# A two-layer AdaLN and FFN kernel: perceptron, attention and aggregated kernels computed beside the last unit, residual rows added by later transfers, the opening in a new order

## The chip, the core and the metric

The kernel is one launch on one core of a Trainium2 chip. The engines run side by side from their own instruction streams: TensorE (PE, with its weight loads shown as PEld), VectorE (DVE), ScalarE (ACT), GpSimd (POOL) and SyncE (SP). SP, ACT and POOL also issue DMA transfers; in the rows their queues are SPq, ACTq and POOLq. Each stream is executed in its own order, and streams wait for each other through semaphores. The metric is the device time of the launch in microseconds (us).

## What is computed

Only what matters here, from the reference; `x` is (32, 64, 1024), 32 batch entries of 64 channels of 1024 values.

```python
# layer 0, condition: grouped 1-d convolution, 9 taps, 4 groups, plus a term per batch entry and channel
out = conv(x, weight, groups=4) + (c @ c_weight.T)[:, :, None] + bias[None, :, None]
# layer 0, FFN on the 2048 rows of 1024: weights are 4-bit codes, looked up and scaled, plus a low-rank part
y1 = x1 @ w_up + b_up + x1 @ w_up_lora_a @ w_up_lora_b
y2 = relu(y1) @ w_down + b_down + relu(y1) @ w_down_lora_a @ w_down_lora_b
# layer 1, condition: a perceptron on the condition gives 8 attention weights per batch entry
h = gelu(embedding @ W0 + b0); h = gelu(h @ W1 + b1); att = softmax(h @ W2 + b2)
agg_w = einsum('bk,koi->boi', att, weight);  agg_b = att @ bias_k
out = einsum('boi,bih->boh', agg_w, x) + agg_b[:, :, None]
# layer 1, FFN: each row goes to the expert (of 8) with the highest gate
yj = xf @ expert_w[j].T + expert_b[j]
```

Layers also add their input (the residual); the kernel holds that sum in `acc`. The perceptron, its attention and the aggregated kernels `agg_w` depend on the condition alone, not on `x`. Their first use is layer 1's mixing of the channels, after the whole FFN of layer 0.

## The kernel before

**Opening.** PE computes the 32 convolutions (one per batch entry, `conv`), each into one of four banks; ACT writes the high part of the result (`conv_high`) and DVE the low part (`conv_low`). Convolution k may start when the low part of k-4 is done. Eight convolutions make one chunk of 512 rows: `stages[0]` to `stages[3]`, the last being the buffer `ring`. POOL stores each finished chunk to DRAM (`store_x1`: 8 transfers of 512 KB, 4 MB in all), since later units read it again. SP loads the inputs of the convolutions in pairs (`load_pair`, 516 KB, into four buffers).

**Weights.** In the same stretch the first weight tiles are decoded. Tile n is a `head` and seven `ramps` on ACT, seven additions on DVE (`add_ramps`), a multiplication by the scales `am` (`scale`), an addition of the low-rank product that PE makes (`lora_product`, `add_lora`), a rounding on ACT (`high`) and a subtraction on DVE (`low`). SP loads codes, scales and low-rank rows (`load_codes`, `load_scales`, `load_lora`); each buffer is loaded again once its last use is past, and SP waits for that in its own order. Tiles 0 and 1 are the "up" tiles of unit 0, tiles 2 and 3 its "down" tiles.

**Main part.** There are 11 units; the 2048 rows are 4 chunks. `up(q)` is 48 products of 128x512 for one chunk, `relu` and `hidden_low` turn its result into hidden values, `down(q)` is another 48 products in four parts j = 0 to 3. DVE adds each part to `acc` (`add_down`), and part j may start when the sum of part j-2 is made (semaphore `acc_added`). PE's order is up(q+1), down(q), up(q+2), and so on. `acc` lies on the memory of `stages[1]` and `stages[2]`. In the kernel before, POOL loads the residual rows `x_nat` into `acc` first (`load_rows`, 16 transfers of 512 KB), once the stage beneath has been used and stored, and `add_down` of unit 0 waits for them (`acc_in`).

**Condition of layer 1.** The ten constants are loaded by ACT's queue at the start. `perceptron(0)` to `perceptron(4)` and eight products `aggregate(j)` stand between convolutions 3 to 15, `aggregated(j)` on ACT copies each result out, and POOL stores the kernels (`batch_kernels<-aggs`, 512 KB). `aggs` and `kerns` lie on `stages[2]`: hence ACT waits for `aggs_stored` before it writes convolution 16.

**After the units** come the mixing of 16 row tiles (`z_product`, with blocks `bdg` loaded from the stored kernels), the gates, the routing and the experts.

The order of all of it is written out by hand, engine by engine, with one loop (`rounds`) for the repeating units. Before the change PE's order in the opening is convolutions 0 to 15, up(0), 16 to 23, up(1), 24 to 31, down(0).

## Time and profile before

| what | value |
|---|---|
| median of 3 runs | 1533.24 us (1530.97 to 1535.55) |
| the profiled execution's own time | 1532.94 us |
| its span in the trace | 1531.5 us |
| PE busy | 1431.8 us, 93% |
| DVE busy | 1125.8 us, 74% |
| ACT busy | 762.1 us, 50% |
| mean granted TensorE clock | 0.974 |
| bytes moved | 331.29 MB, mean 216 GB/s |

Of the 1532.94 us, 1.4 us lie around the span. A busy share is an average over stages; the stages differ, so the profile is read stage by stage. "Idle before" in a row is how long the engine stood still before the instruction, and the name behind the arrow is what ended that wait. A granted clock of 1.00 is 2.4 GHz, of 0.50 it is 1.2 GHz; a value between is a mean over a stretch.

### The profile page before, as it was taken

The page shows a single profiled execution, that of the slowest core. Times are in us where ns is not written, and L with a number is a line of the kernel's source. Part 1 is how long each engine was busy: PE and PEld are TensorE (multiplying, and loading weights), DVE is VectorE, ACT ScalarE, POOL GpSimd, SP SyncE. Part 2 cuts the span into 40 slices and gives each one's busy share as a digit, 9 for nine tenths or more (in the row PEclk, how much of TensorE's full clock was granted, in tenths as well). Part 3 has the DMA queues.
Part 4 walks back from the last instruction along what each step waited for, and adds up shares of the span by engine and source line. Part 5 has one row for each costly group of instructions (what it writes and reads, how often), then busy time and mean ns, then how long its engine had stood idle before and what let it go on. Part 6 is the DMA issues. An engine that isn't in the chain of part 4 may idle for free.

```text
span 1531.5 us, 20837 instructions
## 1 busy us (share of the span) xinstructions
PE 1431.8 (93%) x6815; PEld 1163.4 (76%) x6815; DVE 1125.8 (74%) x1075; ACT 762.1 (50%) x845; POOL 155.1 (10%) x215
## 2 busy tenths in 40 slices
PE   6886899999999999999999999999999499999896
PEld 5576788888888888888888888888865377777674
DVE  3672787877888788787887878875244588888885
ACT  3561554464455455445445445542112266776663
POOL 0112200000000000000000000000011233343440
PEclk8898999999999999999999999999999599999998
DMA  5567565755665665575565566466555845968860
GB/s 163 201 203 277 220 219 219 264 216 194 261 232 193 233 248 199 217 270 189 215 255 223 204 235 254 186 232 212 225 197 211 272 132 138 338 167 248 307 183 2
DMA packets 104365, 331.29 MB, mean 216 GB/s; under 512 B 17361, under 2 KB 24921, under 8 KB 104249
## 3 DMA queue, kind: packets, MB, share of 16 engines
q1 hardware_dynamic: 80478, 258.22, 45.2%
q0 software_dynamic: 22512, 71.32, 15.3%
q8 instruction: 54, 0.88, 0.2%
q10 hardware_dynamic: 1298, 0.68, 0.2%
q14 instruction: 23, 0.18, 0.0%
HBM read 295.04 MB, written 46.14 MB: 223 GB/s over the span
## 4 chain that ended last, share of the span: by engine, by line
PE 82%; DVE 5%; DMA 4%; ACT 3%; issue 3%; ACTq 1%; POOL 1%; DVEq 0%; SPq 0%; POOLq 0%
PE pair L1072 24%; PE pair L1074 23%; PE pair L1073 23%; PE pair L1121 3%; DVE wlr L1046 2%; PE pair L1216 2%; DMA am<-am_dn 1%; PE pair L1281 1%; DMA batch_kernels<-aggs 1%; PE pair L1131 1%; DVE wf L775 1%; ACT whr L707 1%; PE pair L1223 1%; DMA zg<-z_rows,zidx 1%; PE pair L1134 1%
## 5 line engine op out<-in xcount | busy, mean ns | idle before, releaser
L775 DVE TENSOR_TENSOR wf<-wf,term 128x1024 f32<-128x1024 f32 x308 | 377.2, 1225 | 93.4 <-ACT term L568 74.5
L568 ACT ACTIVATE term<-codes 128x1024 f32<-128x1024 int32 x308 | 321.0, 1055 | 107.0 <-DVE wf L775 107.0
L1072 PE MATMUL pair<-wh,hh 128*128 128x512 f32 x704 | 275.2, 391 | 4.0 <-DVE acc L814 2.6
L1074 PE MATMUL pair<-wh,hl 128*128 128x512 f32 x704 | 274.7, 390 | 0.0
L1073 PE MATMUL pair<-wl,hh 128*128 128x512 f32 x704 | 274.6, 390 | 0.0
L1072 PE MATMUL pair<-ring,wh 128*128 128x512 f32 x656 | 255.5, 390 | 1.5 <-issue 1.5
L814 DVE TENSOR_TENSOR acc<-acc,pair 128x1024 f32<-128x1024 f32 x176 | 214.2, 1217 | 57.9 <-PE pair L1074 57.7
L1074 PE MATMUL pair<-ring,wl 128*128 128x512 f32 x656 | 255.2, 389 | 0.0
L1073 PE MATMUL pair<-ring,wh 128*128 128x512 f32 x656 | 255.2, 389 | 0.0
L596 ACT ACTIVATE wh<-wf 128x1024 fp32r<-128x1024 f32 x44 | 46.7, 1060 | 338.7 <-DVE wf L790 338.7
L1046 DVE TENSOR_TENSOR wlr<-wraw,whr 128x1024 fp32r<-128x1024 f32 x184 | 213.1, 1219 | 2.8 <-ACT whr L707 2.8
L707 ACT ACTIVATE whr<-wraw 128x1024 fp32r x184 | 187.9, 1056 | 33.9 <-PE pair L1074 30.7
L1072 PE MATMUL pair<-whr,zth 128*128 128x512 f32 x368 | 151.4, 412 | 21.7 <-DVE wlr L1046 21.7
L1072 PEld LDWEIGHTS pair<-wh,hh 128*128 128x128 f32 x704 | 132.3, 188 | 31.6 <-DVE acc L814 2.7
L1073 PEld LDWEIGHTS pair<-wl,hh 128*128 128x128 f32 x704 | 132.2, 188 | 27.8
L1074 PEld LDWEIGHTS pair<-wh,hl 128*128 128x128 f32 x704 | 132.1, 188 | 27.6
L1073 PE MATMUL pair<-wlr,zth 128*128 128x512 f32 x368 | 144.6, 393 | 0.0
L1072 PEld LDWEIGHTS pair<-ring,wh 128*128 128x128 f32 x656 | 123.1, 188 | 28.1 <-issue 2.7
L1074 PE MATMUL pair<-whr,ztl 128*128 128x512 f32 x368 | 144.4, 392 | 0.0
L1073 PEld LDWEIGHTS pair<-ring,wh 128*128 128x128 f32 x656 | 123.1, 188 | 25.6
L1074 PEld LDWEIGHTS pair<-ring,wl 128*128 128x128 f32 x656 | 123.1, 188 | 25.5
L804 DVE TENSOR_TENSOR hl<-pair,hh 128x1024 fp32r<-128x1024 f32 x44 | 53.9, 1225 | 82.4 <-ACT hh L607 82.4
(165 smaller groups left out, 1386.8 us busy)
## 6 DMA issues: line engine op xcount, KB each, us to landing
ring<-x_parts SPq DMA_DIRECT2D x320, 512.0 KB, 7.7
wraw<-exp_w SPq DMA_DIRECT2D x64, 512.0 KB, 13.1
x_parts<-stage POOLq DMA_DIRECT2D x24, 512.0 KB, 8.5
xg<-exp_b POOLq DMA_DIRECT2D x23, 512.0 KB, 6.9
codes<-codes_up SPq DMA_DIRECT2D x22, 512.0 KB, 7.6
codes<-codes_dn SPq DMA_DIRECT2D x22, 512.0 KB, 6.2
am<-am_dn SPq DMA_DIRECT2D x22, 512.0 KB
acc<-x_nat POOLq DMA_DIRECT2D x16, 512.0 KB, 10.7
```

The lines of the kernel that those rows point to most:

```text
L568: return nc.scalar.activation(out, codes[:, n % 2], ACT.Relu, scale=scale, bias=-scale * bend)
L596: nc.scalar.activation(high_part(n), whole(n), ACT.Copy).then_inc(wh_ready, 1)
L707: nc.scalar.activation(whr[:, kt % 4], wraw[:, bass.ds(buf, 1), kt].rearrange("p a n -> p (a n)"), ACT.Copy).then_inc(whr_ready, 1)
L775: nc.vector.tensor_tensor(whole(n), whole(n), term[:, e % 2], op).then_inc(term_added, 1)
L804: nc.vector.tensor_tensor(hl[:, h:h + 2], pair[0][:].rearrange("p (s t) -> p s t", s=2), hh[:, h:h + 2], ALU.subtract).then_inc(hl_ready, 1)
L814: nc.vector.tensor_tensor(a, a, pair[2 + j % 2][:], ALU.add).then_inc(acc_added, 1)
L1046: nc.vector.tensor_tensor(wlr[:, kt % 4], wraw[:, bass.ds(buf, 1), kt].rearrange("p a n -> p (a n)"), whr[:, kt % 4], ALU.subtract).then_i ...
L1072: mm(ps, ah, bh, start=first, stop=False)
L1073: mm(ps, ah, bl, start=False, stop=False)
L1074: return mm(ps, al, bh, start=False, stop=last)
L1121: ins = mm(whole_bank[:, :, g * GC:(g + 1) * GC], xcv[h][p % 4][:, k % 2, g, d:d + P], tz[h][:, d, g], start=False, stop=g == GROUPS - 1 a ...
L1216: ins = mm(bank[4 * (p % 2) + h], bdg[:, p % 2], rows, start=True, stop=True)
```

## The change

It has four parts.

1. The perceptron, the attention and the aggregated kernels leave the opening. Their constants are loaded by SP near the end of the last decoded tile, the steps stand between the ups and downs of the last unit, the eight products stand two by two behind the four parts of the last unit's down(2), and POOL stores the kernels while down(3) runs. SP loads the first `bdg` blocks only after that store, between the rows 0 to 7 and 8 to 15 of the stores of `acc`.
2. `acc` is no longer loaded with `x_nat` ahead. In unit 0 DVE copies the first four downs into `acc`, and POOL then adds each row tile with an accumulating transfer (`accum_op=ALU.add`), one per finished copy; `add_down` of q = 4 waits for it.
3. The opening's order: convolutions 0 to 20, up(0), convolutions 21 to 23, up(1) with the low-rank product of tile 3 inside, 24 to 31, down(0). The decoding of tiles 0 to 3 is spread over it accordingly.
4. SP's loads in the opening follow that order; the low-rank rows and the scales of tile 3 now stand ahead of the loads of the last four pairs instead of behind.

```diff
-            load_rows(0) ... load_rows(3)      # acc[:, t] <- x_nat, after up_mm and x1_stored
+            for c in range(NC):
+                store_x1(c)
+            for t in range(TILES):
+                pool.wait_ge(acc_added, t + 1)
+                pool.dma_start(acc[:, t], x_nat[t * P:(t + 1) * P], accum_op=ALU.add).then_inc(acc_in[t // CT], 16)
...
-            act.wait_ge(aggs_stored, 16)
-            for k in range(HB, HB + CB):
+            for k in range(FIRST, LATE):
                 conv_high(k)
...
+            sp.wait_ge(term_ready, NCH * WT)
+            for dst, src in ((cta[:], cond_t), (w0s[:], w0), (b0s[:], b0), (w1s[:], w1), (b1s[:], b1), (w2s[:], w2),
+                             (b2s[:], b2), (kernb[:], kern_b), (gbs[:], gate_b)):
+                sp.dma_start(dst, src).then_inc(mlp_const, 16)
+            sp.wait_ge(dn_mm, TILES * (UNITS - 1))
+            sp.dma_start(kerns[:], kern).then_inc(kerns_in, 16)
...
+            store_rows(0)
+            store_rows(1)
+            sp.wait_ge(aggs_stored, 16)
             load_mixing(0, 0)
             load_mixing(0, 1)
+            store_rows(2)
+            store_rows(3)
...
             def add_down(i, q, j):
                 dve.wait_ge(dn_mm, i * 32 + 4 * q + j + 1)
+                a = acc[:, CT * (q % NC) + j]
                 if isinstance(i, int) and i == 0 and q < NC:
+                    dve.wait_ge(up_mm, 2 + q // 2)
+                    dve.wait_ge(x1_stored[1 + q // 2], 16 * KT)
+                    nc.vector.tensor_copy(a, pair[2 + j % 2][:]).then_inc(acc_added, 1)
+                    return
...
             for k in range(NC):
                 if k < NC - 1:
                     up(UNITS // 2, k + 1).then_inc(up_mm, 1)
-                down(UNITS // 2, k)
+                    perceptron(2 * k)
+                down(UNITS // 2, k, aggregates=k == 2)
+                if k < 2:
+                    perceptron(2 * k + 1)
```

How the orders differ at the places that matter. A name such as `early_xcv` is the input of a convolution, `x8` a repeated row. First PE in the opening, convolutions 8 and 9 of the kernel before with what stands around them:

```order
L1096 MATMUL pair<-ident,satt 8x32 [waits mlp_dve]
L1117 MATMUL pair<-ctxd,ones 128x512 [waits x1l_ready,ctxd_ready,xcv_in0]
L1121 MATMUL pair<-tz,xcv 128x8x16 x8
L1099 MATMUL pair<-att_t,kernb 128x32 [waits att_ready]
L1117 MATMUL pair<-ctxd,ones 128x512 [waits x1l_ready]
L1121 MATMUL pair<-tz,xcv 128x8x16 x8
L1105 MATMUL pair<-kerns,att_t 32x512 [waits aggb_ready]
```

and the same convolutions in the changed kernel:

```order
L1129 MATMUL pair<-tz,early_xcv 128x8x16 x8
L1125 MATMUL pair<-ctxd,ones 128x512 [waits x1l_ready,ctxd_ready,xcv_in0]
L1129 MATMUL pair<-tz,xcv 128x8x16 x8
L1125 MATMUL pair<-ctxd,ones 128x512 [waits x1l_ready]
L1129 MATMUL pair<-tz,xcv 128x8x16 x8
L1125 MATMUL pair<-ctxd,ones 128x512 [waits x1l_ready,xcv_in1]
```

Between convolutions PE no longer waits for attention (`satt`, `att_t`, `aggb`). Second, SP's queue before, from the last load of the first 12 pairs to the loads for tile 4:

```order
L304 DMA early_xcv<-x_conv 128x1032 [waits conv_mm]
L366 DMA tz<-toep 128x1024 [waits x1_stored0,up_mm]
L317 DMA lora_raw<-lora_dn_at 96x128 [waits lora_ready]
L304 DMA xcv<-x_conv 128x1032 [waits conv_mm]
L304 DMA late_xcv<-x_conv 128x1032 [waits conv_mm] x3
L310 DMA codes<-codes_up 128x1024 [waits term_ready]
L327 DMA am<-am_dn 128x1x1024 [waits scaled]
L317 DMA lora_raw<-lora_up_b 96x128 [waits lora_ready]
```

and in the changed kernel:

```order
L310 DMA early_xcv<-x_conv 128x1032 [waits conv_mm]
L333 DMA am<-am_dn 128x1x1024 [waits scaled]
L323 DMA lora_raw<-lora_dn_at 96x128 [waits lora_ready]
L333 DMA am<-am_dn 128x1x1024 [waits scaled]
L376 DMA tz<-toep 128x1024 [waits x1_stored0,up_mm]
L310 DMA xcv<-x_conv 128x1032 [waits conv_mm]
L310 DMA late_xcv<-x_conv 128x1032 [waits conv_mm] x3
L316 DMA codes<-codes_up 128x1024 [waits term_ready]
```

The scales of tile 3 (the second `am_dn`) moved from behind the pairs of the last chunk to ahead of them. Third, ACT beside the last unit in the changed kernel, from `relu(1)` to the first of the mixing; before, the same stretch holds the `relu` groups alone:

```order
L612 ACTIVATE pair<-pair,bup 128x512
L617 ACTIVATE hh<-pair 128x1024 [waits relu_done,dn_mm]
L563 ACT_TABLE_LOAD
L563 ACTIVATE hid<-pair,b0s 128x32 [waits mlp_mm]
L566 ACTIVATE hid<-pair,b1s 128x32 [waits mlp_mm]
L612 ACTIVATE pair<-pair,bup 128x512 [waits up_mm]
L612 ACTIVATE pair<-pair,bup 128x512
L617 ACTIVATE hh<-pair 128x1024 [waits relu_done,dn_mm]
L569 ACT_TABLE_LOAD
L569 ACTIVATE satt<-pair,satt 32x8 [waits mlp_dve]
```

The perceptron's steps now stand behind `relu`, and the table load for each stands ahead of the instruction that waits. On PE, the step that needs the attention, between up(3) and down(2) of the last unit:

```order
L1079 MATMUL pair<-ring,wl 128x512
L1106 MATMUL pair<-att_t,kernb 128x32 [waits att_ready]
L1077 MATMUL pair<-wh,hh 128x512 [waits acc_added,hl_ready,wl_ready]
```

Before, the products of down(2) follow those of up(3) with nothing between.

## Rows read from the trace of the kernel before

**Rows 1.** Busy time by stage: us, busy us of each engine, clock, DMA share, GB/s.
```profile
0.00:78.85 78.85, 56.24 (x320) 45.36 (x320) 39.13 (x51) 36.50 (x55) 7.43 (x21) 0.87 0.57 186
78.85:157.28 78.43, 61.72 (x373) 55.63 (x373) 37.61 (x41) 32.02 (x44) 11.00 (x21) 0.87 0.64 225
201.00:1052.00 851.00, 849.54 (x3810) 703.79 (x3809) 684.39 (x605) 435.56 (x489) 0.31 (x1) 1.00 0.60 226
```

**Rows 2.** The chain of work that ended last, in the opening: start, us, what.
```profile
71.85 0.97 PE pair L1105 x2
...
80.86 18.78 DMA batch_kernels<-aggs
...
114.97 22.23 DMA am<-am_dn
```

**Rows 3.** PE in order of time: start, duration, line, operation, idle before.
```profile
10.61 0.77 PE L1117 MATMUL pair<-ctxd,ones 128*128 128x512 f32 x1 [4.00 <-DVE ctxd L759]
...
14.13 0.48 PE L1117 MATMUL pair<-ctxd,ones 128*128 128x512 f32 x1
...
16.15 0.47 PE L1117 MATMUL pair<-ctxd,ones 128*128 128x512 f32 x1
```

**Rows 4.** PE, the same view: a wait for the perceptron, a low-rank product.
```profile
26.23 0.41 PE L1089 MATMUL pair<-hid,w1s 128*128 128x32 f32 x2 [3.55 <-ACT hid L553]
...
65.50 1.11 PE L1131 MATMUL pair<-lora_t,lora 96*128 96x128 f32 x8
```

**Rows 5.** PE, the same view: up(0), up(1), convolution 28, down(0).
```profile
78.85 0.79 PE L1072 MATMUL pair<-stage,wh 128*128 128x512 f32 x1 [0.68 <-ACT aggs L564]
...
91.89 0.39 PE L1117 MATMUL pair<-ctxd,ones 128*128 128x512 f32 x1
...
113.85 0.48 PE L1072 MATMUL pair<-stage,wh 128*128 128x512 f32 x1
...
124.87 0.39 PE L1117 MATMUL pair<-ctxd,ones 128*128 128x512 f32 x1
...
145.05 0.76 PE L1117 MATMUL pair<-ctxd,ones 128*128 128x512 f32 x1 [11.95 <-DVE ring L819]
...
157.28 0.50 PE L1072 MATMUL pair<-wh,hh 128*128 128x512 f32 x1 [1.41 <-DVE ring L819]
```

**Rows 6.** DVE in order of time, in the opening, columns as for PE.
```profile
80.92 1.23 DVE L775 TENSOR_TENSOR wf<-wf,term 128x1024 f32<-128x1024 f32 x1 [3.05 <-ACT term L568]
...
91.80 1.22 DVE L790 TENSOR_TENSOR wf<-wf,pair 128x1024 f32<-128x1024 f32 x1
...
138.55 1.22 DVE L790 TENSOR_TENSOR wf<-wf,pair 128x1024 f32<-128x1024 f32 x1
...
144.22 2.47 DVE L819 TENSOR_TENSOR ring<-pair,ring 128x512 fp32r<-128x512 f32 x4
```

**Rows 7.** Transfers by issue, 43 to 44 and 74 to 77 us: KB each, us to landing.
```profile
early_xcv<-x_conv SPq DMA_DIRECT2D x1, 516.0 KB, 7.8
...
early_xcv<-x_conv SPq DMA_DIRECT2D x1, 516.0 KB, 17.2
```

**Rows 8.** ACT and DVE in order of time, at `relu(2)` of the last unit.
```profile
1084.00 1.24 ACT L602 ACTIVATE pair<-pair,bup 128x512 f32<-128x512 f32 x2 [19.41 <-PE pair L1074]
1085.33 1.03 ACT L607 ACTIVATE hh<-pair 128x1024 fp32r<-128x1024 f32 x1
...
1087.53 1.21 DVE L814 TENSOR_TENSOR acc<-acc,pair 128x1024 f32<-128x1024 f32 x1
1089.34 1.22 DVE L814 TENSOR_TENSOR acc<-acc,pair 128x1024 f32<-128x1024 f32 x1 [0.60 <-PE pair L1074]
```

**Rows 9.** ACT in order of time: table load, first perceptron step.
```profile
24.59 1.28 ACT L553 ACT_TABLE_LOAD   x1
25.89 0.29 ACT L553 ACTIVATE hid<-pair,b0s 128x32 f32<-128x32 f32 x1
```

**Rows 10.** The page's transfers by issue: an accumulating one, KB each, median us to landing.
```profile
xg<-exp_b POOLq DMA_DIRECT2D x23, 512.0 KB, 6.9
```

More of the change, by code:

```diff
@@ L171, in program @@
         term = sb(late, "term", [P, 2, L])
+        cta = sb(tail, "cta", [P, P])
+        w0s = sb(tail, "w0s", [P, P])
+        w1s = sb(tail, "w1s", [P, P])
+        w2s = sb(tail, "w2s", [P, E])
+        b0s = sb(tail, "b0s", [P, 1])
+        b1s = sb(tail, "b1s", [P, 1])
+        b2s = sb(tail, "b2s", [1, E])
+        kernb = sb(tail, "kernb", [E, P])
+        hid1 = sb(tail, "hid1", [P, B])
+        hid2 = sb(tail, "hid2", [P, B])
+        satt = sb(tail, "satt", [B, 3 * E])
+        tail.close()
         codes = sb(late, "codes", [P, 2, L], I32)
@@ L345, in _ @@
             load_pair(1)
+            load_pair(2)
             load_lora(0, 0)
+            load_scales(0, 0)
+            load_pair(3)
             load_codes(0, 1)
-            load_scales(0, 0)
-            for p in range(2, 6):
-                load_pair(p)
+            load_pair(4)
             load_lora(0, 1)
+            load_pair(5)
             load_pair(6)
-            load_codes(0, 2)
             load_scales(0, 1)
             load_pair(7)
+            load_codes(0, 2)
+            load_pair(8)
             load_lora(0, 2)
-            load_pair(8)
             load_pair(9)
+            load_pair(10)
             load_codes(0, 3)
-            load_pair(10)
+            load_pair(11)
             load_scales(0, 2)
-            load_pair(11)
+            load_lora(0, 3)
+            load_scales(0, 3)
             sp.wait_ge(up_mm, 1)
@@ L613, in conv_high @@
                                      ACT.Copy).then_inc(x1h_ready, 1)
-            act.wait_ge(ffn_const, 32)
-            for k in range(HB):
+            for k in range(FIRST):
                 conv_high(k)
@@ L675, in _ @@
             high(UNITS // 2, 3)
-            for k in range(3):
-                relu(UNITS // 2, k + 1)
+            relu(UNITS // 2, 1)
+            perceptron(0)
+            perceptron(1)
+            relu(UNITS // 2, 2)
+            perceptron(2)
+            relu(UNITS // 2, 3)
+            for j in range(8):
+                aggregated(j)
             act.wait_ge(aggb_ready, 2)
@@ L808, in add_down @@
                 dve.wait_ge(dn_mm, i * 32 + 4 * q + j + 1)
+                a = acc[:, CT * (q % NC) + j]
                 if isinstance(i, int) and i == 0 and q < NC:
-                    dve.wait_ge(acc_in[q], 16 * CT)
-                else:
-                    dve.wait_ge(acc_added, i * 32 + 4 * (q - NC) + j + 1)
-                a = acc[:, CT * (q % NC) + j]
+                    dve.wait_ge(up_mm, 2 + q // 2)
+                    dve.wait_ge(x1_stored[1 + q // 2], 16 * KT)
+                    nc.vector.tensor_copy(a, pair[2 + j % 2][:]).then_inc(acc_added, 1)
+                    return
+                if isinstance(i, int) and i == 0:
+                    dve.wait_ge(acc_in[q - NC], 16 * CT)
+                dve.wait_ge(acc_added, i * 32 + 4 * (q - NC) + j + 1)
                 nc.vector.tensor_tensor(a, a, pair[2 + j % 2][:], ALU.add).then_inc(acc_added, 1)
@@ L820, in conv_low @@
                                         stages[c][:, :, 0, col:col + CH], ALU.subtract).then_inc(x1l_ready, 1)
-            for k in range(HB):
+            for k in range(FIRST):
                 conv_low(k)
@@ L866, in _ @@
             add_lora(0, 2)
+            low(0, 2)
             dve.wait_ge(up_mm, 1)
@@ L870, in _ @@
             hidden_low(0, 0)
-            for k in range(HB, HB + CB):
+            for k in range(FIRST, LATE):
                 conv_low(k)
-                if k < HB + 7:
-                    add_ramps(0, 3, (k - HB + 1,))
-                if k == HB + 1:
-                    lora_low(0, 3)
-                    low(0, 2)
+            add_ramps(0, 3, (1,))
+            lora_low(0, 3)
+            add_ramps(0, 3, range(2, 8))
             scale(0, 3)
@@ L881, in _ @@
             hidden_low(0, 1)
-            for k in range(HB + CB, B):
+            for k in range(LATE, B):
                 conv_low(k)
@@ L910, in _ @@
                     hidden_low(UNITS // 2, k + 1)
+                if k == 1:
+                    perceptron(0)
+                    perceptron(1)
+                elif k == 2:
+                    perceptron(2)
+                    perceptron(3)
                 for j in range(CT):
@@ L1157, in up, with down @@
                 return ins
-            def down(i, q, between=None):
+            def down(i, q, between=None, aggregates=False):
                 pe.wait_ge(wl_ready, i * 8 + 4 * (q // 4) + 4)
```

200 lines of the change are left out of this document (77 added, 123 removed).

## The prediction, made before the changed kernel had run

> **What bounds the kernel now.** I read the busy time by stage first. From 201 us on PE is busy without a gap and at full clock, for 850 us of a main part that the change leaves alone, and the same holds up to 1127 us [rows 1]. The opening is different: in its two halves PE is busy for 56.2 of 78.9 and 61.7 of 78.4 us, at a granted clock of 0.87, and DVE and ACT are below half [rows 1]. No engine bounds the opening; waits do. So I read the chain of waits there. Two single transfers hold 41.0 us of it: the store of the aggregated kernels (18.8 us), for which ACT waits before convolution 16, and the scales of tile 3 (22.2 us) [rows 2]. The second ends in PE standing still for 11.95 us before convolution 28 [rows 5]. Before those two, PE waits for the perceptron between convolutions, as the 3.55 us at 26.2 us [rows 4]. The goal of the reading is one time: down(0) of unit 0 starts at 157.28 us [rows 5]. From there both kernels have the same order of work on PE, DVE and ACT, until the last unit.
>
> **The opening, step by step.** The costs: the first convolution takes 14.13 - 10.61 = 3.5 us, a later one 16.15 - 14.13 = 2.02 us [rows 3]; a low-rank product of the up kind 1.1 us [rows 4]. DVE needs 0.62 us for a low part (2.47 for four) and 1.22 us for one operation on a weight tile [rows 6], 1.84 us together, and the new order gives it one such operation per convolution: PE's 2.02 us is the longer. The start hardly moves: ACT issues ten transfers less, but the convolution also needs its input, and I take 10.5 us instead of 10.61.
> Convolutions 0 to 20 then end at 10.5 + 3.5 + 20 x 2.02 + 2 x 1.1 = 56.6 us. I add 1.5 us for a late input (below): 58.1.
> up(0) needs the low part of tile 1, which now comes last: after convolution 20 one ACT copy and three DVE operations (0.6 + 0.6 + 2 x 1.2 with the hand-overs), 3.8 us. PE stands still for that, so up(0) starts slowly, as it did before: 91.89 - 78.85 = 13.0 us with its slow start and one low-rank product [rows 5]. It ends at 74.9.
> Convolutions 21 to 23: 6.1, to 81.0. `relu(0)` and its low part are done by then (74.9 + 3.6, the time from `relu` to the first addition in [rows 8]), so up(1) runs at once: 124.87 - 113.85 = 11.0, plus 0.5 for the product inside, to 92.5 [rows 5]. Convolutions 24 to 27 need nothing more: to 100.6.
> Convolution 28 needs the low part of 24, and DVE is the later one there. Tile 3: ACT writes convolution 23 and the head and first ramp of tile 3 by 83.7; from the first addition to the end of `add_lora` it took 93.0 - 80.9 = 12.1 us for tile 2 with nothing between [rows 6], so 95.9; from there to the end of `hidden_low` 144.2 - 139.8 = 4.4, so 100.3, and 0.7 for the low part: 101.0. Convolutions 28 to 31 end at 109.1, and the last low part brings down(0) to 110.8 (before: 1.7 us behind the last convolution).
> **Term of the opening: 157.3 - 110.8 = 46.5 us less.** The 22 us wait for scales goes because SP now issues that load right behind `scale` of tile 2 (about 72 us), 22 us before it is needed and before the store of the next chunk; what is late next is DVE's tile 3, as computed.
>
> **The residual rows.** 16 plain loads leave (two groups of eight, one of them beside the late scales), and 16 accumulating ones come, one per copied tile, some 5.5 us apart. DVE's copy in place of the sum reads the same 1024 values; I cost it at nothing. The trace has one accumulating transfer of the same size, 6.9 us to landing [rows 10]. The last of a group is issued as its down ends; it is needed when the same rows come again four steps later, 3 x 22 us at least. So it is hidden by the main part; if it were not, `add_down(4)` would stall. POOL has nothing else queued there. Bounds: 0 to 3 us, for loads of the ring that it delays; I take 0.
>
> **The last unit.** Here PE has no gap, so what is put on it costs in full. Eight aggregated products at 0.97 us [rows 2]: 7.8. The perceptron's six small ones, from 0.1 to 0.4 us each: 1.2. Then waits. perceptron(0) and (1) find their inputs ready: ACT works them off beside a down or an up of 11 us, and the nine constants were issued a down and an up before. perceptron(4) stands between up(3) and down(2) and needs the attention that DVE copies after `hidden_low(3)`: `relu` to the first addition is 1087.5 - 1084.0 = 3.5 us [rows 8], plus the copy and the step: 3.9 us in which PE stands still, and then a slow start, priced by the two ups: 13.0 - 11.0 - 0.5 = 1.5 us [rows 5]. Behind it down(2), the `relu` after it and everything later wait. In down(1) DVE does the softmax between `hidden_low` and its first sum. Part 2 of down waits for that sum; it is ready at 1088.7 and wanted at 1089.3 [rows 8]. The softmax puts about 1.5 us in (two small operations, the exponential, two more), less 0.4 us by which PE is later itself: 0.5 us. The table load for the exponential (1.28 us [rows 9]) stands ahead of the waiting instruction, from 1086.3 on, beside `hidden_low`.
> In [rows 9] the instruction behind a table load starts 0.02 us after it. The Trainium skill (ScalarE: Activation LUTs, What ACT_TABLE_LOAD costs) counts a drain of 1.38 us on top, 2.66 us per switch. The row speaks against this; by the page the sum would be about 1.4 us higher.
> The kernels' store is issued behind the last aggregated product, while down(3) runs for 11 us. The 18.8 us that it took before had 4 MB of other stores ahead on the same queue; now nothing is ahead. With some 4 us, and 4 us for the blocks, it is hidden; bounds 0 to 8 us, I take 0.
> **Term of the last unit: 7.8 + 1.2 + 3.9 + 1.5 + 0.5 = 14.9 us more.**
>
> **Sum.** 1532.94 - 46.5 + 14.9 = 1501.3 us. The median of the runs, 1533.24, is 0.3 us above the profiled execution: 1501.5.
>
> **The rivals.**
> *The opening becomes short of transfers.* The first store of 4 MB now starts at about 30 us, and the pairs for convolutions 14 and 16 are issued at 34 to 35 us beside it. The pair for 14 is wanted at 41.3. Such a pair took 7.8 us beside the first store before and 17.2 beside the second [rows 7]: ready at 42 or at 51. I took 1.5 us, near the first row, since that one also was issued just behind a store's start. With the second PE would lose 10 us and 1.5 for the slow start: 1511.
> The Trainium skill (DMA: Bandwidth & Descriptors, Queues, rings and completion order) says that each DMA engine goes round-robin between queues, by packets. By that rule a pair would never wait for the whole store, and the 1.5 us would fall away; the 17.2 us row speaks against it.
> *The clock does not recover.* If convolutions with short waits keep PE at the mean 0.87 of now, 2.02 us becomes 2.3: 32 convolutions and two ups cost 12 us more, 1513. For it: waits of 1 to 2 us are followed by slow stretches now. Against it: from 14.13 us on, without waits, the pace is 2.02.
> *The accumulating transfers hold the main part up (slower than before).* Their place is the wait of `add_down(4)` to `(7)` in unit 0. Group 0 is wanted 3 x 22 = 66 us after its last issue, group 3 seven steps, 154 us, after down(0). If the sixteen went one behind another they would be late at all from 154 / 16 = 9.6 us each, and would eat the 31.6 us won from 11.6 us each; at 12.5 us each, 200 - 154 = 46 us late, 1547. For it: nothing in the trace shows sixteen of them in a row. Against it: one lands 6.9 us after its issue, beside other transfers, and transfers overlap.
> *The condition's work is not in the way before.* If DVE and ACT set the opening and not its waits, the gain is one of the two transfers only, some 22 us, with 15 given back: 1526. Rows 1 speak against it, both are half idle.
>
> **How the numbers follow.** Forecast (1494 to 1508) 0.68; short of transfers 0.12; clock 0.10; gain of one transfer only 0.04; accumulating transfers 0.04; nothing moves 0.02. The lower end is the forecast with no late input, a hidden softmax and no slow start, and a start 3 us earlier, and DVE 2 us quicker over tile 3: 1493. The upper end takes in the first two rivals and the 8 us of the store's bound in part: 1515. A measurement of this kernel tells 0.3% (4.6 us) from no change. Faster by more than that: all but the last two cases, 0.94; within: 0.02; slower: 0.04.
>
> **What would show it.** Down(0) starts near 111 us, at a clock above 0.95 in the first 58 us; no wait of DVE for `am`; no wait of ACT for `batch_kernels`; a gap of 3 to 4 us on PE ahead of perceptron(4) and a last unit longer by 15 us; DVE never waits for `acc`'s accumulating transfers. Wrong are I if PE waits for a pair of inputs at convolutions 14 to 20, if DVE is late at convolution 28 by more than a microsecond, or if the first `bdg` block comes after down(3).

## The result, and the profile after

| | median | runs |
|---|---|---|
| before | 1533.97 us | 4 (1530.97 to 1535.55) |
| changed | 1548.21 us | 4 (1546.64 to 1552.64) |

The ratio is 1.0100, with a 95% interval of 1.0074 to 1.0126: the changed kernel is 14 us slower. Forecast was 1501.5, with a range that ended at 1515. The profiled execution of the changed kernel took 1546.64 us, its span is 1545.2. All comparisons of places below are made in the spans, 1545.2 against 1531.5: 13.7 us. One of the four executions of the kernel before with the scales on 16 engines, an experiment below, took 2918.49 us and is left out of that kernel's median, 1510.03 us; two expectations still count it and write 1511.2.

The stages first (us; busy us of each engine, clock, DMA share, GB/s), beside [rows 1]:

```profile
0.00:66.44 66.44, 50.26 (x377) 48.56 (x377) 42.09 (x51) 36.38 (x50) 9.45 (x24) 0.95 0.72 260
66.44:124.23 57.79, 49.42 (x287) 43.63 (x287) 34.19 (x35) 26.01 (x34) 4.19 (x8) 0.91 0.49 174
125.00:250.00 125.00, 105.65 (x452) 84.80 (x451) 85.29 (x76) 52.93 (x59) 17.54 (x24) 0.96 0.85 235
250.00:1052.00 802.00, 799.98 (x3588) 663.22 (x3587) 637.19 (x564) 405.96 (x456) 0.31 (x1) 1.00 0.60 224
```

The opening is shorter and denser, and from 250 us on the main part runs without a gap as before. The third row is new: 19 us of PE are missing in the first 125 us of the main part, at a DMA share of 0.85 and yet only 235 GB/s. What PE waited for in the whole kernel (us in all, times, longest), the rows that concern the change. L1077 holds products of an up or a down, L1125 opens a convolution, L1222 is the mixing, L1106 the step that needs the attention:

```profile
PE pair L1077 <- DMA ring<-x_parts: 16.8, 7, 7.7
PE pair L1125 <- DMA xcv<-x_conv: 9.6, 2, 6.4
PE pair L1222 <- DMA bdg<-batch_kernels: 7.8, 1, 7.8
...
PE pair L1125 <- DMA early_xcv<-x_conv: 4.0, 1, 4.0
PE pair L1106 <- DVE att_t L746: 3.9, 1, 3.9
PE pair L1077 <- DVE wl L806: 3.7, 1, 3.7
```

Four of the six are transfers (3.2 of the 9.6 us are the first convolution's, at the start). In order of time on PE: convolution 14, up(0), up(1), convolution 24, down(0), beside [rows 5]:

```profile
44.73 0.80 PE L1125 MATMUL pair<-ctxd,ones 128*128 128x512 f32 x1 [4.01 <-DMA early_xcv<-x_conv]
...
66.44 0.51 PE L1077 MATMUL pair<-stage,wh 128*128 128x512 f32 x1 [3.68 <-DVE wl L806]
...
86.40 0.47 PE L1077 MATMUL pair<-stage,wh 128*128 128x512 f32 x1 [0.55 <-issue]
...
104.48 0.80 PE L1125 MATMUL pair<-ctxd,ones 128*128 128x512 f32 x1 [6.41 <-DMA xcv<-x_conv]
...
124.23 0.50 PE L1077 MATMUL pair<-wh,hh 128*128 128x512 f32 x1 [1.41 <-DVE ring L831]
```

The chain of work that ended last, its four longest transfers up to 260 us (start, us, what), beside [rows 2]:

```profile
33.80 10.88 DMA early_xcv<-x_conv
...
81.55 22.90 DMA xcv<-x_conv
...
173.45 27.18 DMA ring<-x_parts
...
207.84 27.54 DMA ring<-x_parts
```

Three transfers of half a megabyte took 23 to 28 us each, and they set the end. The difference of the two spans, by stage:

| stretch | before | changed | difference |
|---|---|---|---|
| start to down(0) of unit 0 | 157.28 | 124.23 | -33.0 |
| down(0) to `relu(1)` of the last unit (its `hh` copy at 1063.56 and 1053.65) | 906.28 | 929.42 | +23.1 |
| from there to the last sum into `acc` (1127.42 and 1133.59) | 63.86 | 79.94 | +16.1 |
| last sum to the end | 404.1 | 411.6 | +7.5 |
| sum | | | +13.7 |

In the last stretch the third `z` tile comes 9.3 us later after the last sum than before (1149.50 - 1133.59 = 15.9 against 1134.05 - 1127.42 = 6.6 us), and 1.8 us come back behind it (9.3 - 7.5).

**Who holds the transfers up.** The loads on SP's queue around the late one of convolution 24:

```profile
80.47 0.52 SPq L333 DMA_DIRECT2D am<-am_dn  x1
81.11 0.39 SPq L376 DMA_DIRECT2D tz<-toep  x1
81.55 0.43 SPq L310 DMA_DIRECT2D xcv<-x_conv  x1
```

The load that lands late stands behind the scales of tile 3, which the change moved ahead of it. Two windows of the changed kernel in which such a load of scales, the one of tile 2, is alone in flight (last two columns: DMA share, GB/s):

```profile
70.00:73.00 3.00, 3.00 (x13) 2.43 (x12) 2.79 (x3) 2.47 (x3) 0.00 (x0) 0.82 0.13 52
73.00:78.00 5.00, 5.00 (x23) 4.12 (x22) 1.50 (x2) 0.04 (x1) 0.00 (x0) 1.00 0.13 52
```

A share of 0.13 of 16 engines is two engines, busy without a break, at 26 GB/s each; 512 KB take 10 us of both. The access pattern is two rows of DRAM, each to 64 partitions (`broadcast_to([2, 64, L])`). The Trainium skill (DMA: Bandwidth & Descriptors, Why a DMA increments its semaphore by 16 and not by 1) says that a transfer is spread over the largest number of engines, up to 16, that divides the slowest dimension of both patterns; by that rule a slowest dimension of 2 gives two engines, and the trace agrees with it: a share of 0.13.

What this does to the loads behind shows after the scales of tile 3 have landed. DVE, which waited for them, goes on at 99.48 us. The loads issued after them, from 82 to 88 us, are still in flight (median us to landing of each kind), and the window in which they end has the same two busy engines:

```profile
99.48 1.23 DVE L792 TENSOR_TENSOR wf<-wf,am 128x1024 f32<-128x1024 f32 x1 [1.43 <-DMA am<-am_dn]
...
late_xcv<-x_conv SPq DMA_DIRECT2D x3, 516.0 KB, 26.1
codes<-codes_up SPq DMA_DIRECT2D x1, 512.0 KB, 28.2
...
107.00:110.00 3.00, 3.00 (x20) 2.96 (x20) 0.64 (x1) 0.60 (x1) 0.00 (x0) 0.73 0.13 53
```

No load of a down tile's scales is in flight there. So two engines still work at the rest of the later loads while the other fourteen are idle: each of those loads has a part on the two, and lands only when that part has.

The queues of the changed kernel from 125 to 250 us (packets, MB, share of 16 engines; then the transfers, KB each, median us to landing):

```profile
q0 software_dynamic: 3456, 12.58, 44.7%
q1 hardware_dynamic: 5408, 16.67, 39.6%
...
ring<-x_parts SPq DMA_DIRECT2D x24, 512.0 KB, 23.3
acc<-x_nat POOLq DMA_DIRECT2D x16, 512.0 KB, 9.3
```

and in the same stretch of the kernel before, where POOL's queue moves plain loads and stores:

```profile
q0 software_dynamic: 4181, 15.20, 32.4%
...
ring<-x_parts SPq DMA_DIRECT2D x23, 512.0 KB, 9.4
```

POOL's queue needs 12.58 MB / (0.447 x 16 x 125 us) = 14 GB/s of an engine's time where it had 15.20 / (0.324 x 16 x 125) = 23. The accumulating transfers cost the engines more, and loads of `ring` take 23 us instead of 9.

### The profile page after: what moved, and what is told of

Same layout as the page of the kernel before. It is cut to its first block, busy times and chain, and to the rows that moved or that the text cites. A ratio compares the mean times of both kernels' runs of the same rounds, so it can differ in the third digit from the quotient of the medians.

```text
span 1545.2 us, 20837 instructions
## 1 busy us (share of the span) xinstructions
PE 1433.3 (93%) x6815; PEld 1161.2 (75%) x6815; DVE 1126.2 (73%) x1075; ACT 763.8 (49%) x845; POOL 155.1 (10%) x215
## 4 chain that ended last, share of the span: by engine, by line
PE 81%; DMA 8%; DVE 5%; ACT 2%; issue 2%; SPq 1%; ACTq 1%; DVEq 0%; POOL 0%; POOLq 0%
PE pair L1077 24%; PE pair L1078 23%; PE pair L1079 23%; DMA ring<-x_parts 4%; PE pair L1129 3%; DMA xcv<-x_conv 2%; DVE wlr L1051 2%; PE pair L1222 2%; PE pair L1287 1%; DMA wraw<-exp_w 1%; PE pair L1139 1%; ACT whr L714 1%; PE pair L1229 1%; DVE wf L782 1%; DMA early_xcv<-x_conv 1%
## 5 line engine op out<-in xcount | busy, mean ns | idle before, releaser
L1077 PE MATMUL pair<-wh,hh 128*128 128x512 f32 x704 | 277.6, 394 | 3.9 <-DVE acc L821 2.5
L1077 PE MATMUL pair<-ring,wh 128*128 128x512 f32 x656 | 257.7, 393 | 18.8 <-DMA ring<-x_parts 16.8
L826 DVE TENSOR_TENSOR acc<-acc,pair 128x1024 f32<-128x1024 f32 x160 | 194.7, 1217 | 68.8 <-PE pair L1079 68.7
L1077 PE MATMUL pair<-whr,zth 128*128 128x512 f32 x368 | 151.9, 413 | 21.5 <-DVE wlr L1051 21.4
L1077 PEld LDWEIGHTS pair<-ring,wh 128*128 128x128 f32 x656 | 123.7, 189 | 48.8 <-DMA ring<-x_parts 12.1
L1077 PEld LDWEIGHTS pair<-wh,hh 128*128 128x128 f32 x704 | 133.2, 189 | 35.5 <-DVE acc L826 2.9
L1078 PEld LDWEIGHTS pair<-wl,hh 128*128 128x128 f32 x704 | 132.9, 189 | 27.5
```

Source lines behind the costliest of these rows:

```text
L826: nc.vector.tensor_tensor(a, a, pair[2 + j % 2][:], ALU.add).then_inc(acc_added, 1)
L1077: mm(ps, ah, bh, start=first, stop=False)
L1078: mm(ps, ah, bl, start=False, stop=False)
```

## The experiments

Two things are suspected, the scales on two engines and the accumulating transfers, and the runs take them apart in both kernels. Ratios, where one is given, are to the kernel before in runs on the same chip; a time without one is that of a single execution. The kernel before took 1531.1 to 1534.0 us (medians) in the five series, so a difference of 3 us between kernels of different series says nothing.

**The changed kernel with scales on 16 engines.** The two rows are held eight times each in DRAM; the transfer reads 16 rows, each to 8 partitions, and moves the same bytes.

```diff
-                                 .broadcast_to([2, 64, L])).then_inc(am_in, 16)
+                                 .broadcast_to([16, 8, L])).then_inc(am_in, 16)
...
-        am_up=au, am_dn=ad, ...
+        am_up=au, am_dn=np.repeat(ad, 8, axis=1), ...
```

> The changed kernel, with one edit: the scales of the down tiles (am_dn, 512 KB per load) are laid out with each row eight times, so that a load reads 16 rows spread 8 ways instead of 2 rows spread 64 ways. In the trace of the changed kernel such a load alone moves 52 GB/s at a DMA share of 0.13 (70 to 78 us), which is 2 of 16 engines. Theory A (two engines): every later load has a part on those two engines and waits behind the scales there, and this is why loads of the ring land after 23 to 27 us and the pair for convolution 24 after 22.9. Then with this edit: PE's waits for ring and for convolution 24 fall from 16.8 and 6.4 us to under 3 in all, DVE's waits for am from 15.9 to under 2, and the time by 28 to 36 us, to about 1516. Theory B (the accumulating transfers alone hold the engines): the waits for ring stay within a few us of 16.8, only those for am go, and the time falls by under 12 us, to 1536 or more.

Measured: 1515.89 us, ratio 0.9901 (0.9869 to 0.9932), 32 us below the changed kernel. No wait for `ring` or `am` is left on PE and DVE, the scales land in 4.5 us (median), down(0) starts at 113.9 us instead of 124.2, and the main part's 23 us are gone. The accumulating transfers are still there, at 8.3 us each, and alone they hold nothing up that PE or DVE would wait for.

**The kernel before, the same edit.**

> The kernel before, with the same edit of the scales' layout alone. Its late transfers in the opening were the scales of tile 3 (landing after 22.2 us) and the store of the aggregated kernels (18.8 us). Theory A: DVE's wait of 21 us for am shrinks to under 5 us (the load shares 16 engines with 8 MB of stores and rows then in flight), and the time falls by 8 to 16 us, since PE lost 12 us ahead of convolution 28 and the clock. Theory B (bytes in front of it, not the number of engines): the wait stays over 15 us and the time within 3 us of 1534.

Measured: 1510.03 us (1509.10 to 1512.35), ratio 0.9859 (0.9818 to 0.9899). The kernel before had lost 21 us to the same load, more than the 8 to 16 expected. The 11.95 us wait of [rows 5] is gone; of the 21.0 us that DVE waited for `am` 6.0 are left, a little over the 5 expected. Down(0) starts at 138.7 instead of 157.3. With the scales mended in both, the changed kernel is still 5.9 us slower; its opening gains 24.8 us (138.7 against 113.9), its last unit and the mixing give back more.

**Residual rows by plain transfers.** The changed kernel; order, waits and the bytes read stay, only the adding goes, so this kernel leaves the first four downs out of its result.

```diff
-                pool.dma_start(acc[:, t], x_nat[t * P:(t + 1) * P], accum_op=ALU.add).then_inc(acc_in[t // CT], 16)
+                pool.dma_start(acc[:, t], x_nat[t * P:(t + 1) * P]).then_inc(acc_in[t // CT], 16)
```

> The changed kernel with the 16 accumulating transfers of the residual rows made plain loads at the same places: acc is overwritten, so the result lacks the first downs; bytes, queue and times of issue are the same. Theory B (accumulating itself, at about half the rate of a plain transfer by engine time): the waits for ring fall from 16.8 us to under 6 and the time by 12 to 20 us. Theory A alone (scales on two engines): waits stay at 12 to 18 us. Theory C (8 MB more at that place, whatever their kind): as A, no change.

Measured: 1534.39 us, 14 below the changed kernel; from down(0) to `relu(1)` of the last unit it needs 917.1 us (1039.73 - 122.65). PE waits for `ring` once, 7.1 us, instead of seven times and 16.8 us; the ring loads take 10.3 us instead of 23.3, and POOL's queue moves its 12.17 MB at a share of 28.1% instead of 44.7% (22 GB/s an engine).

**No residual rows at all.** The sixteen transfers and the wait for them are left out, and with them the residual.

> The changed kernel without the 16 transfers of the residual rows and without the wait for them: the residual is left out of the result. It gives the whole price of these transfers in the main part. Theories B and C: the waits for ring go to 0 to 3 us and the time falls by 18 to 24 us, to about 1525. Theory A alone: ring loads still stand behind the scales on two engines, but these drain twice as fast with nothing beside them, so the waits fall to under 8 us and the time by 8 to 16 us.

Measured: 1525.09 us, 23 below the changed kernel, with no wait for `ring`. The same stretch needs 907.6 us (1031.00 - 123.45) instead of 929.4: 21.9 of the main part's 23.1 us are gone. With scales on two engines the rows thus cost this stretch 9.5 us as plain loads and 21.9 us as accumulating ones; with scales on 16 engines they cost nothing that shows.

**The late rows alone, on the kernel before.** Opening, perceptron and attention stay as they were.

```diff
-            pool.wait_ge(up_mm, 2)
-            pool.wait_ge(x1_stored[1], 16 * KT)
-            load_rows(0)
-            load_rows(1)
             store_x1(3)
-            pool.wait_ge(up_mm, 3)
-            pool.wait_ge(x1_stored[2], 16 * KT)
-            load_rows(2)
-            load_rows(3)
+            for t in range(TILES):
+                pool.wait_ge(acc_added, t + 1)
+                pool.dma_start(acc[:, t], x_nat[t * P:(t + 1) * P], accum_op=ALU.add).then_inc(acc_in[t // CT], 16)
```

(`add_down` of unit 0 copies first, as in the change.)

> The kernel before with one part of the change alone: the first writes of the residual copy, and the rows come by accumulating transfers behind them. Opening, perceptron and attention stand where they stood. Theory (an accumulating transfer takes about twice the engine time, and on queues already held up by the two-engine scales that turns into waits for ring tiles): the main part waits for ring tiles 5 to 17 us, and the time is 1536 to 1550. Rival (the 23 us that the main part lost came from the new opening, which ends nearer to the first loads, and the rows cost nothing): 1529 to 1533, with no ring wait behind the first matmul of down(0).

Measured: 1555.01 us, ratio 1.0129 (1.0097 to 1.0161): 22.6 us slower than before, beyond the end of what was expected (three executions took 1554.8 to 1555.9 us, the fourth 1546.6), and by this part of the change alone. Waits of PE, and of DVE for the scales:

```profile
PE pair L1067 <- DMA ring<-x_parts: 17.8, 7, 7.3
PE pair L1112 <- DVE ring L814: 11.6, 1, 11.6
...
DVE wf L776 <- DMA am<-am_dn: 33.9, 4, 20.6
```

The second row is the old wait of [rows 5]. From down(0) to the last sum this kernel needs 1152.3 - 159.1 = 993.2 us; before it was 970.1. The 23 us of the changed kernel are here without its opening.

**The same with scales on 16 engines.**

> The run before with scales that use 16 engines. Theory (only the two together hurt): no wait for a ring tile in the main part, and 1508 to 1514, level with the kernel before with the same scales (1511.2). Rival (the accumulating rows cost by themselves): 1518 to 1530.

Measured: 1509.66 us, no wait for a ring tile, and 969.6 us from down(0) to the last sum. That is level with the 1510.03 us of the kernel before with the same scales: the rows are free once the scales are mended, in this kernel too.

**Two engines, or two rows of DRAM?** The copy of the rows changed both. In this run the same two rows are read, by two transfers of one row to 64 partitions.

```diff
-                    sp.dma_start(am[:], am_dn[bass.ds(t, 1)].rearrange("a k (o n) -> (a k) o n", o=1)
-                                 .broadcast_to([2, 64, L])).then_inc(am_in, 16)
+                    for k in range(2):
+                        sp.dma_start(am[64 * k:64 * k + 64], am_dn[bass.ds(t, 1), k].broadcast_to([64, L])).then_inc(am_in, 16)
...
-                dve.wait_ge(am_in, i * 128 + 16 * (n + 1))
+                dve.wait_ge(am_in, i * 192 + 96 * (n // 4) + (16, 32, 64, 96)[n % 4])
```

> The changed kernel, with the scales of a down tile fetched by two transfers of one row to 64 partitions each, in place of one transfer of two rows to 128. The rows in DRAM are the same two and the bytes are the same; only the number of engines that share one transfer can differ. Theory (a transfer with two rows slowest in its walk is spread over two engines): as with the scales laid out in 16 rows, 1513 to 1519, no wait for a ring tile, scales landing in under 10 us. Rival (two rows of DRAM read 64 times over are slow from any number of engines): 53 GB/s stays, the ring waits stay near 17 us, and the time stays in 1540 to 1552.

Measured: 1515.64 us, ratio 0.9886 (0.9869 to 0.9902), level with 1515.89. The median landing of the two is 3.8 us, and no ring wait is left. How often a row of DRAM is read does not matter; over how many engines the walk is spread does.

**Four rows.** The rows are held twice each, four rows to 32 partitions.

> The changed kernel with the scales' rows held twice each in DRAM, four rows to 32 partitions each. Theory (engines as rows): alone in flight the scales' load moves about 106 GB/s at a DMA share of 0.25, twice that of two rows; an own busy time of 5 us against 10 leaves part of the hold-up: ring waits 0 to 8 us, 1516 to 1535. If the number of rows did not set the rate, 53 GB/s and 1544 to 1552.

Measured: 1528.07 us. A window with the load alone in flight:

```profile
70.00:72.00 2.00, 2.00 (x11) 1.62 (x10) 1.90 (x2) 1.74 (x2) 0.00 (x0) 1.00 0.26 98
```

Four of sixteen engines, twice the rate of two rows, and of the ring waits 8.0 us are left. Two, four and sixteen engines give 1548, 1528 and 1516 us.

**The order of the last stores.** SP in the changed kernel, from the first blocks `bdg` on:

```profile
1127.50 2.95 SPq L403 DMA_DIRECT2D bdg<-batch_kernels  x4
1130.49 8.16 SPq L409 DMA_DIRECT2D x_rows<-acc  x8
1139.02 25.86 SPq L403 DMA_DIRECT2D bdg<-batch_kernels  x14
```

Row tiles 8 to 11 of `acc` have been ready since 1121.9 us (the last sum of down(2) starts at 1120.65 and takes 1.22), but SP stands before them and waits for the kernels; then eight row tiles go out in one piece, 4 MB, and the second pair of blocks is behind them. The next run changes this order alone.

```diff
             store_rows(1)
+            store_rows(2)
             sp.wait_ge(aggs_stored, 16)
             load_mixing(0, 0)
             load_mixing(0, 1)
-            store_rows(2)
             store_rows(3)
```

> The changed kernel with one line of SyncE's list moved: rows 8 to 11 of the residual are stored before SyncE's wait for the aggregated kernels' store, not behind the first two pairs of mixing kernels. In the changed kernel rows 8 to 15 (4 MB) went out in one burst, and L1222 then waited 7.8 us for a pair of kernels. Theory (the burst holds up the kernels behind it): the wait falls to 0 to 4 us and the time by 4 to 9 us, to 1539 to 1544. Rival (the kernels are late because the first mixing stage itself starts late and the queue has too much to do in any order): the wait stays at 7 to 9 us or moves to the first pair, and the time stays within 2 us of 1548.

Measured: 1537.66 us, ratio 1.0035 (1.0023 to 1.0048), a little better than expected. The wait at L1222 fell from 7.82 to 0.34 us, as two rows on PE show, first the changed kernel's:

```profile
1145.68 3.78 PE L1222 MATMUL pair<-acc,bdg 128*128 128x512 f32 x4 [7.82 <-DMA bdg<-batch_kernels]
```

and with the order changed:

```profile
1138.00 1.98 PE L1222 MATMUL pair<-acc,bdg 128*128 128x512 f32 x4 [0.34 <-DMA bdg<-batch_kernels]
```

The first also shows the slow clock behind a long wait: 3.78 us for what takes 1.98, at a granted clock of 0.50 (from 1145.68 to 1149.40 us).

**Both edits, on the changed kernel.**

> Both edits on the changed kernel: the scales are laid out for 16 engines, and rows 8 to 11 are stored early. With the scales alone 1515.9 was measured and the wait for a pair of mixing kernels was 8.4 us. If the burst theory holds, 1507 to 1511, which is level with the kernel before with the same scales (1511.2). If the rival of the run before holds, 1515 to 1517.

Measured: 1506.33 us, ratio 0.9829 (0.9812 to 0.9845). That is 3.7 us below the kernel before with the same scales (1510.03). The two were measured on different chips and the intervals of their ratios overlap (0.9812 to 0.9845, 0.9818 to 0.9899), so with its two faults mended the change is at best a small gain, and this one is not shown.

**A third edit: two copies on DVE.** PE's 3.9 us wait in the last unit had been forecast, and the question is whether it must be. DVE in the run before, start, us, idle before:

```profile
1067.28 1.23 DVE L811 TENSOR_TENSOR hl<-pair,hh 128x1024 fp32r<-128x1024 f32 x1 [12.48 <-ACT hh L617]
1068.42 0.17 DVE L746 COPY att_t<-pair 8x32 f32<-8x32 f32 x1
```

DVE had stood idle for 12.48 us with the attention ready in its bank, since the copy of it is written behind the low part of the last hidden tile.

```diff
             for k in range(NC):
+                if k == 2:
+                    perceptron(2)
+                    perceptron(3)
                 if k < NC - 1:
                     hidden_low(UNITS // 2, k + 1)
                 if k == 1:
                     perceptron(0)
                     perceptron(1)
-                elif k == 2:
-                    perceptron(2)
-                    perceptron(3)
```

> The changed kernel with three edits: the scales in 16 rows, residual rows 8 to 11 stored ahead of the wait for the kernels, and in the last unit VectorE's copies of the attention (L746) and of the bias (L751) ahead of the low parts of the last hidden tile, not behind them. TensorE waited 3.9 us for L746 only because VectorE was itself waiting for ScalarE's last hidden tile. With the first two edits 1506.3 was measured. Theory: the wait goes and nothing takes its place, 1500.5 to 1503.5 (3.9 us, and up to 1.5 more since the matmuls behind it then need not run up from a low clock). Rival (the low parts of the hidden tile come as much later as the wait was long): 1505 to 1507.

Measured: 1499.94 us, ratio 0.9789 (0.9773 to 0.9806). PE waits for nothing in the last unit. The gain is 6.4 us, more than was expected. A window behind the wait, clock in the third column from the end, first with the wait:

```profile
1069.00:1074.00 5.00, 5.00 (x13) 3.93 (x13) 0.34 (x2) 0.00 (x0) 0.00 (x0) 0.50 0.00 0
```

and then without:

```profile
1069.00:1074.00 5.00, 5.00 (x17) 2.52 (x16) 1.75 (x2) 1.17 (x2) 0.00 (x0) 1.00 0.26 105
```

From the last `hidden_low` to the last sum it is 35.0 us with the wait (1102.31 - 1067.28) and 28.1 without (1095.74 - 1067.64). The wait itself was 3.9 of the 6.9 us, the half clock behind it 3.0. How long the half clock lasts behind the same wait differs: in the changed kernel it is over at about 1105.3 us, 4 us after the wait's end, and there the same stretch, 33.6 us (1133.59 - 1099.96), is 5.5 us longer than without the wait.

**A fourth edit: the first store later.** This asks what held the input of convolution 14 up.

```diff
-                pool.wait_ge(x1l_ready, CB * (c + 1))
+                pool.wait_ge(x1l_ready, CB * (c + 1) if c else 13)
```

> The kernel with three edits (1499.9) and one more: the store of the first chunk of convolved rows (4 MB on GpSimd's queue) waits for convolution 13 and not for convolution 8. In the changed kernel and in the one with three edits the input of convolution 14 was issued at 34.1 and took 10.7 us to land, beside that store, and TensorE waited 3.9 us and then ran 16 matmuls at a low clock. Theory (the store takes the engines from that load): the load lands within 7 us, the wait goes, up(0) starts 4 to 5 us earlier, and the time is 1494.5 to 1497.5. Rival (the store then holds up the inputs of convolutions 18 to 22 in the same way, or VectorE's terms set the start of up(0) whatever TensorE does): up(0) stays within 1.5 us of 69, and the time is 1498.5 to 1502.

The bound of 69 us in it was misread: up(0) starts at 65.23 us in the run before. Measured: 1492.84 us, ratio 0.9744 (0.9728 to 0.9761), 7.1 us less, on another chip, and more than was expected; the spans of the profiled executions differ by 5.3 us (1498.1, 1492.8), and that much the steps below account for. The load of convolution 14 in a window around its issue, first beside the store:

```profile
early_xcv<-x_conv SPq DMA_DIRECT2D x1, 516.0 KB, 10.7
```

and with the store behind it:

```profile
early_xcv<-x_conv SPq DMA_DIRECT2D x1, 516.0 KB, 4.2
```

The wait is gone and up(0) starts 5.3 us earlier, at 59.88; the last sum comes 5.5 us earlier. Down(0):

```profile
110.20 0.50 PE L1077 MATMUL pair<-wh,hh 128*128 128x512 f32 x1 [1.41 <-DVE ring L831]
```

This is the fastest of all kernels here, 2.6% faster than the kernel before, 3.6% than the changed one, and 1.1% than the kernel before with the scales mended, beyond the intervals of both ratios.

| kernel | us | down(0) starts | last sum |
|---|---|---|---|
| before | 1533.97 | 157.3 | 1127.4 |
| changed | 1548.21 | 124.2 | 1133.6 |
| before, scales on 16 engines | 1510.03 | 138.7 | 1108.7 |
| changed, scales on 16 engines | 1515.89 | 113.9 | 1102.2 |
| the same, rows 8 to 11 earlier | 1506.33 | 114.2 | 1102.3 |
| the same, attention copied earlier | 1499.94 | 114.2 | 1095.7 |
| the same, first store later | 1492.84 | 110.2 | 1090.3 |

## Why the prediction was wrong, step by step

**The step that failed first: the residual rows, term 0 with bounds 0 to 3; measured 23 us.** Landing times of 6.9 us [rows 10] were compared with the time until the rows are needed, and that part was right: DVE never waits for them. What was not costed is what they take from the engines for everybody else. The bound "0 to 3 us, for loads of the ring that it delays" named the right victim and gave no number from a row for it. The rival on the slower side even ended at 1547 us, but its mechanism (`add_down(4)` waits for late rows) did not happen; that its figure lies near the result is chance. The runs name the cause: accumulating transfers (14 against 23 GB/s of an engine's time) on top of two engines that the scales already fill. Without the other each costs the main part next to nothing: 907.6 us without the rows and 907.3 with scales on 16 engines, where the kernel before has 906.3.

**The opening, 46.5 us forecast; 33.0 measured.** The 13.5 us that are missing stand at three places. Convolution 14 waited 4.0 us for its input, for which 1.5 had been taken, and ran 16 matmuls in 3.41 us instead of 1.78 behind the wait, so up(0) started at 66.4 and not at 61.9: 4.5 us. From there to up(1) 0.9 more, 20.0 against 19.1, with DVE waiting 4.6 us for the scales of tile 2 inside up(0). Convolution 24 waited 6.4 us, with a slow start behind it. That is the failing argument: "the 22 us wait for scales goes because SP now issues that load" earlier. The load was treated as something that comes late; it is something that blocks, 10 us of two engines, and 22 us in all when others are in the way. Issued earlier, it stood in front of the inputs of the last chunk instead of behind them. [rows 2] show its 22.23 us, and the trace of the kernel before has a window in which such a load is alone:

```profile
196.00:200.00 4.00, 4.00 (x19) 3.30 (x19) 2.15 (x3) 3.66 (x5) 0.00 (x0) 1.00 0.13 53
```

The question "why does half a megabyte take 22 us" was never asked. The rival "short of transfers" had the right kind of wait and 0.12; it looked at convolution 14 alone, not at 24.

The engines' own work was sized rightly. With scales on 16 engines and the first store out of the way nothing in the opening waits for a transfer behind the start, and the steps come where the sum had them:

| | forecast | changed kernel | with the four edits |
|---|---|---|---|
| up(0) starts | 61.9 | 66.4 | 59.9 |
| up(1) starts | 81.0 | 86.4 | 80.1 |
| down(0) starts | 110.8 | 124.2 | 110.2 |

The clock (the rival with 0.10) recovers: it is 0.99 up to up(0) in the last column's run and 0.95 in the changed kernel, with the wait of convolution 14. That DVE and ACT do not set the opening held as well.

**The last unit, 14.9 us forecast; 16.1 measured.** Right, and in its parts: PE waited 3.9 us at L1106. The slow start behind it was taken at 1.5 us and measures 1.6 here: the kernel with three edits, which has no wait, needs 74.4 us for the stretch (1095.74 - 1021.32), the changed one 79.9. The other 1.1 us are in the products, the small steps and the softmax: 74.4 - 63.9 = 10.5 us, for which 7.8 + 1.2 + 0.5 = 9.5 had been taken. ACT at the softmax:

```profile
1077.01 1.28 ACT L569 ACT_TABLE_LOAD   x1
1078.51 0.26 ACT L569 ACTIVATE satt<-pair,satt 32x8 f32<-32x8 f32 x1 [0.22 <-DVE satt L736]
```

The table load is 1.28 us, and 0.22 us later the exponential starts, released by DVE. The reading of [rows 9] holds for this place too. The drain of 1.38 us that the Trainium skill (ScalarE: Activation LUTs, What ACT_TABLE_LOAD costs) adds is not seen in this row either. But the 3.9 us was taken as a price of the change. It was one of the order that DVE's list had, and three lines moved took it away.

**The kernels' store hidden, bounds 0 to 8; measured: hidden itself, 9.3 us behind it.** It landed in 4.1 us, as forecast. The bound looked at the first blocks `bdg`, which came in time; the second pair was behind 4 MB of rows that SP, waiting for that store, had let pile up. What is queued behind the waiting instruction was looked at for the first load and not for the next.

**Sum.** -33.0 + 23.1 + 16.1 + 9.3 - 1.8 = 13.7 us, against -46.5 + 14.9 = -31.6. Of the 45.3 us between them 13.5 are the opening's, 23.1 the main part's and 9.3 the mixing's, 1.2 the last unit's, less 1.8. The first three are all late transfers; spreading the scales over 16 engines alone takes back 32 us (1548.21 to 1515.89), and what it leaves is the wait of convolution 14 and the mixing's. The prediction's own sum gives 1501.3 + 0.3 = 1501.6 and not 1501.5, which changes nothing.

**What stays open.** From down(0) to `relu(1)` of the last unit the changed kernel with scales on 16 engines still needs 1.2 us more than the kernel before with the same scales (907.3 against 906.1 us). Both wait about 2.5 us for DVE's sum or copy at the same place, 31.8 us behind the start of down(0) (145.75 and 170.58 us); around it the granted clock is 0.72 in the one (144 to 150 us) and 1.00 in the other (165 to 185 us), which is enough for the 1.2 us; why it falls in only one is not shown. Which two engines serve the scales, and how one engine divides its time between the two queues, is not shown by a view used here; that an accumulating transfer's cost falls on those two in particular is argued from the runs, not seen.

## What to carry to other kernels

Before a load is moved earlier, ask what it does to those behind it: divide its bytes by its landing time, and look at a window in which it is alone; a share of 0.13 at 53 GB/s is a transfer on two of sixteen engines, and the repair is in its access pattern, not in its place. A transfer that nobody waits for still has a price, the engine time that it takes, so cost added transfers by the share of their queue and not by their own landing. And where an engine waits for a value that another has long had in reach, look at what stands before the copy in that engine's list.

## What the runs showed of the hardware

- A broadcast load whose access pattern has two rows slowest uses two DMA engines, 52 to 53 GB/s in all; with four rows 98 to 104 GB/s at a share of 0.26 to 0.27; with 16 rows, or one row to 64 partitions, it lands in 3.8 to 4.5 us. Reading the same DRAM rows more often made no difference (1515.64 and 1515.89 us).
- With such loads on the queue, transfers of about 512 KB issued behind them took 20.8 to 28.2 us in the opening and, as the ring loads on the chain, 27.2 and 27.5 us; with the scales on 16 engines the ring loads' median is 7.3 to 8.1 us. After the scales had landed, two engines were still busy alone (share 0.13) with what was left of the later loads.
- Accumulating transfers (DRAM rows added into SBUF) took a queue share of 44.7% for 12.58 MB, plain ones 28.1% for 12.17 MB over the same 125 us: about 1.5 times the engine time for a queue that holds 4 MB of stores besides. With the scales on 16 engines it is no less: 36.4% for 8.81 MB.
- After PE had stood still for 3.9 us, the granted clock was 0.50 for the next 5 us, and the wait cost 6.9 us in all (the changed kernel with two edits); the same wait cost 5.5 us in the changed kernel, where the clock was back sooner.
